# Two-layer perceiver, self-attention's maxima: bf16 parts instead of f32 rows, and zero products in the open sums

## What is computed

```python
x = x + L0_xattn(layernorm(x), ctx, mask, ...)       # 16 heads x 8, 2048 keys
x = x + L0_attn(layernorm(x), W_dq, W_uq, ...)       # causal: keys k <= query q
x = x + L0_ffn(layernorm(x), ...)
x = x + L1_xattn(layernorm(x), ctx, ctx, ...)
x = x + L1_attn(layernorm(x), attn_w, attn_b, ...)
x = x + L1_ffn(layernorm(x), ...)                    # 16 experts, 4 chosen

# L1_attn: masked scores are set to -10000 and kept in the softmax
scores = where(k <= q, k.q / sqrt(8), -10000.0); probs = softmax(scores, over k); out = probs @ v
```

## Time and profile before

| | us |
|---|---|
| median of 3 runs | 305.57 |
| lowest, highest | 305.34, 307.09 |
| the profiled execution's own time | 305.52 |
| its span | 303.5 |
| TensorE busy (share of the span) | 284.2 (94%) |
| VectorE busy | 227.0 (75%) |
| ScalarE busy | 206.4 (68%) |
| GpSimd busy | 68.7 (23%) |
| mean granted TensorE clock | 0.989 |

### The profile page before, as it was taken

One profiled execution on the slowest core, in us unless ns is written; L12 is line 12 of the kernel. 1 busy time (PEld: TensorE's weight loads), 2 busy tenths in 40 slices (PEclk: granted clock), 3 DMA queues, 4 the chain that ended last, 5 costly groups with the idle time before them and its releaser, 6 DMA issues.

```text
span 303.5 us, 10281 instructions
## 1 busy us (share of the span) xinstructions
PE 284.2 (94%) x4324; PEld 185.0 (61%) x4329; DVE 227.0 (75%) x371; ACT 206.4 (68%) x436; POOL 68.7 (23%) x135
## 2 busy tenths in 40 slices
PE   7957999999999999899989899999999999999995
PEld 5444666667676664453745567666666765436575
DVE  6944889999999983563638999999999970643583
ACT  5656689898998987524433698998989987133350
POOL 6793500110101003520000676001011021110001
PEclk9996999999999999999999999999999999999999
DMA  7973415532222450333100025522221100000000
GB/s 229 409 282 123 158 55 171 184 102 77 80 80 82 139 217 2 121 140 104 55 2 0 3 65 181 176 81 82 71 83 60 56 3 2 0 2 3 0 0 19
DMA packets 10898, 28.06 MB, mean 92 GB/s; under 512 B 2241, under 2 KB 3329, under 8 KB 10466
## 3 DMA queue, kind: packets, MB, share of 16 engines
q1 hardware_dynamic: 10776, 27.16, 26.6%
q10 hardware_dynamic: 74, 0.20, 0.2%
HBM read 20.74 MB, written 6.62 MB: 90 GB/s over the span
## 4 chain that ended last, share of the span: by engine, by line
PE 71%; DVE 15%; DMA 5%; ACT 3%; POOL 2%; issue 2%; SPq 1%; ACTq 1%; DVEq 0%; POOLq 0%
PE bank L1040 70%; DVE mx L812 10%; DMA ctxT_s<-in_ctxT 2%; DMA k_first_rows<-kparts 2%; DMA kpair<-k_first_rows 1%; ACT probs L545 1%; DVE s_neg L867 1%; POOL m_rows L427 1%; DVE negm L819 1%; ACTq L276 1%; DVE st L723 1%; DVE kparts L782 0%; PE bank L1336 0%; DVE k_rest L779 0%; POOL m_rows L429 0%
## 5 line engine op out<-in xcount | busy, mean ns | idle before, releaser
L812 DVE TENSOR_REDUCE mx<-bank 128x2 f32<-128x1024 f32 x128 | 153.0, 1222 | 16.1 <-PE bank L1040 12.7
L545 ACT ACTIVATE probs<-bank 128x512 f32<-128x512 f32 x256 | 139.3, 595 | 20.1 <-PE bank L1040 16.1
L1040 PE MATMUL bank<-q_exp,kpair 64*128 64x128 bf16 x1024 | 84.7, 218 | 1.9 <-ACT probs L545 1.2
L1040 PE MATMUL bank<-probs,v_all 128*9 128x128 f32 x2048 | 80.3, 274 | 1.1 <-ACT probs L545 1.0
L1040 PE MATMUL bank<-kpair,q_rows 64*128 64x512 bf16 x256 | 73.7, 387 | 5.6 <-DMA kpair<-k_first_rows 5.1
L1040 PEld LDWEIGHTS bank<-q_exp,kpair 64*128 64x128 bf16 x1024 | 55.3, 94 | 31.6 <-issue 12.7
L1040 PEld LDWEIGHTS bank<-probs,v_all 128*9 128x9 f32 x2048 | 43.2, 90 | 16.7 <-ACT probs L545 4.0
L427 POOL CAST m_rows<-negm 128x2 bf16<-128x2 f32 x32 | 6.9, 217 | 144.6 <-DVE negm L819 144.6
L1040 PEld LDWEIGHTS bank<-kpair,q_rows 64*128 64x128 bf16 x256 | 22.7, 93 | 7.4 <-issue 5.5
L482 ACT ACTIVATE v_all<-bank 128x512 f32<-128x512 f32 (+1 forms) x20 | 10.5, 539 | 13.3 <-PE bank L1040 13.3
L1040 PE MATMUL bank<-selq,ident_b 128*128 128x512 bf16 x70 | 17.8, 379 | 0.3
(11 more groups left out here) (219 smaller groups left out, 341.9 us busy)
## 6 DMA issues: line engine op xcount, KB each, us to landing
k_scratch<-kparts SPq DMA_DIRECT2D x24, 256.0 KB, 2.9
kpair<-k_scratch SPq DMA_DIRECT2D x62, 96.0 KB
kpair<-k_scratch SPq DMA_DIRECT2D x62, 64.0 KB
ctxT_s<-in_ctxT SPq DMA_DIRECT2D x4, 512.0 KB, 6.0
mask_s<-in_mask SPq DMA_DIRECT2D x2, 1024.0 KB, 10.3
kpair<-k_scratch SPq DMA_DIRECT2D x62, 32.0 KB
wM<-in_packM SPq DMA_DIRECT2D x1, 1728.0 KB, 7.0
wB<-in_packB SPq DMA_DIRECT2D x1, 599.0 KB, 5.0
```

The source lines that it names most:

```text
L545: act.activation(probs[:, j % 4, :], bank[:, 4 + j % 2, :], ACT.Exp).then_inc(S("exp_done"), 1)
L812: V.tensor_reduce(mx[n % 2][:, w, :], bank[:, 2 * (w % 2):2 * (w % 2) + 2, :], AX.X, ALU.max) \
L1040: return T.matmul(out_, lhsT=lhsT, rhs=rhs, start=start, stop=stop, **kw)
```

## The change

The maxima now go into a small contiguous f32 tile `s_neg` of 16 numbers a partition and batch. A new VectorE step `split_max(b)` splits them into three bf16 parts at stride 32 of a cleared bf16 tile `s_parts` (four operations on 128x16, each waiting for the one before). `neg_rows(b)` waits for the split and is four plain bf16 products with the bf16 identity; the three parts of a maximum land in three rows of its group, the 29 others are zero. `s_row` becomes bf16, `subtract(b)` a bf16 product that adds the three rows up. GpSimd clears `s_parts` and fills `ones_b` and `zero_b` in place of clearing `s_neg`. ScalarE's `exp_fill` reads the new `s_neg`.

On TensorE, `later(0, 0..2)` moves to the front and `neg_rows(0)` behind `scores(1)`; `later(1, 0..2)` moves ahead of `neg_rows(1)`. A new `hold(b, g, n)` adds n products of the zero tile with 512 columns of `selq` to an open sum: four after `later(0, 0..2)`, four after `later(1, 0..2)`, two after `turned(1, 0..2)`, in each of the two layers. On VectorE, `split_max(0)` stands behind `expand_k(l, 1)` and `split_max(1)` behind `s_max(1, 1)`.

```diff
-        s_neg = sb("s_neg", [P, B, 4 * (P + 1)])
-        s_row = wide[:, 6:8, :].rearrange("p b (j q) -> p b j q", j=4)
+        s_neg = sb("s_neg", [P, B, 4, 4])
+        s_rest = sb("s_rest", [P, B, 4, 4])
+        s_parts = sb("s_parts", [P, B, 4, P], BF16)
+        ones_b = sb("ones_b", [P, P], BF16)
+        zero_b = sb("zero_b", [P, P], BF16)
+        s_row = wide[:, 6, :].bitcast(BF16).rearrange("p (b j q) -> p b j q", b=B, j=4)
...
+        def part_of(b, k):
+
+            return s_parts[:, b, :, :].rearrange("p j (g r) -> p g j r", r=32)[:, :, :, k]
...
-                        pool.memset(s_neg[:, :, :], 0.0).then_inc(S("neg_zero"), 1)
+                        pool.memset(s_parts[:, :, :, :], 0.0).then_inc(S("neg_zero"), 1)
+                        pool.memset(ones_b[:, :], 1.0).then_inc(S("neg_zero"), 1)
+                        pool.memset(zero_b[:, :], 0.0).then_inc(S("neg_zero"), 1)
...
+                def split_max(b):
+
+                    if l == 0 and b == 0:
+                        dve.wait_ge(S("neg_zero"), 1)
+                    dve.wait_ge(S("s_neg"), 2 * l + b + 1)
+                    link(V.tensor_copy(part_of(b, 0), s_neg[:, b, :, :]))
+                    link(V.tensor_tensor(s_rest[:, b, :, :], s_neg[:, b, :, :], part_of(b, 0), ALU.subtract))
+                    link(V.tensor_copy(part_of(b, 1), s_rest[:, b, :, :]))
+                    V.tensor_tensor(part_of(b, 2), s_rest[:, b, :, :], part_of(b, 1), ALU.subtract) \
+                        .then_inc(S("s_split"), 1)
...
                 expand_k(l, 1)
+                split_max(0)
                 for i in range(2):
                     s_max(1, i)
+                split_max(1)
                 dve.wait_ge(S("neg_t"), 2 * l + 2)
...
                 def neg_rows(b):
 
-                    pe.wait_ge(S("s_neg"), 2 * l + b + 1)
+                    pe.wait_ge(S("s_split"), 2 * l + b + 1)
                     for j in range(4):
-                        last = T.transpose(bank[:, S_BANK[b][3], j * P:(j + 1) * P],
-                                           s_neg[:, b, j * P:(j + 1) * P], ident)
+                        last = mm(bank[:, S_BANK[b][3], j * P:(j + 1) * P], s_parts[:, b, j, :], ident_b[:, :])
                     last.then_inc(S("neg_t"), 1)
...
+                def hold(b, g, n):
+
+                    for _ in range(n):
+                        mm(bank[:, S_BANK[b][g], :], zero_b[:, :], selq[:, 0:512], start=False, stop=False)
+
                 def subtract(b):
 
                     for g in range(4):
-                        mm(bank[:, S_BANK[b][g], :], ones_sq[group(g), :],
+                        mm(bank[:, S_BANK[b][g], :], ones_b[group(g), :],
...
-                neg_rows(0)
+                if l == 0:
+                    pe.wait_ge(S("neg_zero"), 3)
+                later(0, range(3))
+                hold(0, 0, 4)
                 pe.wait_ge(S("k_s"), 2 * l + 2)
                 pe.wait_ge(S("q_s"), 2 * l + 2)
                 pe.wait_ge(S("v32"), 2 * l + 2)
...
                 mask(1, 0, range(4))
                 scores(1)
-                later(0, range(3))
+                neg_rows(0)
                 turned(0, range(3))
                 later(0, range(3, 4))
                 turned(0, range(3, 4))
                 subtract(0)
+                later(1, range(3))
+                hold(1, 0, 4)
                 neg_rows(1)
-                later(1, range(3))
                 turned(1, range(3))
+                hold(1, 0, 2)
                 later(1, range(3, 4))
                 turned(1, range(3, 4))
                 subtract(1)
```

More of the change, by code:

```diff
@@ L245, in x_before @@
             return len(X_UNIT) * l + sum(u < n for u in X_UNIT)
-        def s_max_of(b):
-            v = s_neg[:, b, :].rearrange("p (j r) -> p j r", j=4)[:, :, 0:P]
-            return v.rearrange("p j (g r) -> p g j r", r=32)[:, :, :, 0]
+        def part_of(b, k):
+            return s_parts[:, b, :, :].rearrange("p j (g r) -> p g j r", r=32)[:, :, :, k]
         def r_bank(k):
@@ L607, in exp_fill @@
                     act.activation(e_fill[:, b, :].rearrange("p (g j) -> p g j", g=4),
-                                   s_max_of(b), ACT.Exp,
+                                   s_neg[:, b, :, :], ACT.Exp,
                                    bias=B_("fill", 1)).then_inc(S("e_fill"), 1)
@@ L864, in s_max @@
                         dve.wait_ge(S("sa_done"), 2 * l + b + 1)
-                    if l == 0 and b == 0 and i == 0:
-                        dve.wait_ge(S("neg_zero"), 1)
-                    last = V.tensor_reduce(s_max_of(b)[:, 2 * i:2 * i + 2, :],
+                    last = V.tensor_reduce(s_neg[:, b, 2 * i:2 * i + 2, :],
                                            bank[:, S_BANK[b][2 * i]:S_BANK[b][2 * i] + 2, :].rearrange("p g (j k) -> p g j k", j=4),
@@ L871, in s_max @@
                         link(last)
-                        last = V.tensor_scalar(s_max_of(b), s_max_of(b), B_("nfill", 1), None, ALU.min)
+                        last = V.tensor_scalar(s_neg[:, b, :, :], s_neg[:, b, :, :], B_("nfill", 1), None, ALU.min)
                     if i:
                         last.then_inc(S("s_neg"), 1)
+                def split_max(b):
[7 more added lines that the diff above has]
+                        .then_inc(S("s_split"), 1)
                 def finish(b):
```

## The result

| | before | changed |
|---|---|---|
| first session: median, us (lowest, highest) | 305.70 (305.34, 307.09) | 308.77 (307.75, 309.43) |
| ratio, 95% interval | | 1.0091 [1.0065, 1.0117] |
| second session: median, us | 306.62 | 308.76 |
| ratio, 95% interval | | 1.0071 [1.0046, 1.0097] |
| span of the profiled execution, first and second session | 303.5 | 307.2, 305.4 |

The change made the kernel slower by 2 to 3 us where I had forecast 0.3 us less. The time is outside the range.

A forecast was written before the change was run, and what follows sets the result against it. TensorE's serial sequence in two self-attention stretches was taken as the bound; bf16 savings nearly all spent on 2.16 us of holds a layer left 0.12 + 0.18 = 0.30 us gained, so 305.3 us, range 304.3 to 306.7.

The forecast's parts named there:

- The place: TensorE's stretch in both self-attentions, 10.18 and 10.24 us; each microsecond earlier there is a microsecond off the end.
- the wait for v32: TensorE's wait for ScalarE's v32, 0.25 us in the first stretch and 0.31 in the second, was to go.
- the step of a zero product: Hold products on TensorE: 0.216 us each from the trace, 2.16 us for the ten of a layer.
- The 131 ns of the Trainium skill: Rejected price per 512-column hold product: ten would cost 1.31 us, gaining some 1.7 us more over both layers.
- The step that failed: End of each stretch: exponentials start no later than before, so the values' products, reaching the last group 1.6 us in, follow TensorE.
- the last of the signs of being wrong: Values' products that start on time while their end waits for ScalarE's exponentials; listed as showing the forecast wrong.
- 10.06: Forecast stretch up to the values' products, us, from 10.18 and 10.24: gains of 0.12 and 0.18.
- The subtractions of batch 0 with what follows: Batch 0's last turned product and bf16 subtractions, with batch 1's masks starting beside: 1.07 us, bounds 1.07 and 1.40.
- The split's 0.84 us: VectorE's four split operations: 0.84 us, bounds 0.7 and 1.4; batch 0's was to fall into 1.45 us of idleness.
- the turns' +0.28: Upper bound on four bf16 turns of the maxima: 0.60 us against 0.32 taken, twice a layer.
- the subtractions' +0.33 and +0.12: Upper bounds on the last turned product with bf16 subtractions: 1.40 against 1.07 and 1.40 against 1.28, once a layer each.
- a fallen clock: Rival: a wait of microseconds drops TensorE to 1.2 GHz in a stretch, 308.6 us and more; chance 0.05.

The follow-up runs named there:

- Experiment 4: Changed kernel without holds, split_max(0) ahead of expand_k(l, 1), subtractions of groups 0 to 2 ahead of the last masks and turned product; ratio 1.0009 against the kernel before.
- experiment 8: Changed kernel without its first four holds (after the first twelve masks); stretches 13.03 and 13.29 us in one profile, against 13.17 and 13.29 with all holds.
- experiment 9: Changed kernel with split_max(0) ahead of expand_k(l, 1) and only four holds, behind batch 1's first masks; ratio 1.0017 in both runs; also reviews clock falls without holds.
- experiment 2: Changed kernel with all ten holds of each layer taken out; ratio 0.9972 against the kernel before, stretches 11.63 and 12.00 us.
- experiment 5: Changed kernel without holds, early subtractions, first half of batch 0's split ahead of the keys' expansion, the rest behind; 304.77 us, ratio 0.9961 against the kernel before.
- experiment 6: Changed kernel with early subtractions, batch 0's split halved around the keys' expansion, one zero product behind the first twelve masks; ratio 0.9964 against the kernel before.

## Why the prediction was wrong

**What held.** The place (two stretches, all serial behind them), the clock (1.00 in both with the holds, 0.989 over all), the bf16 turns (0.32 each, predicted 0.32), no wait ahead of the turns of batch 1, the wait for v32 gone. The trace was right about the step of a zero product: the second four take 0.87 us, 0.86 predicted. The 131 ns of the Trainium skill (TensorE: Matmul & The Clock Gate, Back-to-back issue gap) would have made them 0.52, and these rows do not agree with it.

**The step that failed.** "ScalarE's exponentials start no later than before, and the values' products reach the last group 1.6 us after their start, so they follow TensorE." I let the bf16 subtractions of groups 0 to 2, which run beside the turned product of group 3, signal ScalarE at once. Their completion reaches it 1.16 us after that product's start, as late as with f32 (1.17). So the 0.65 us saved behind it in batch 1 brought the values' products forward and not the exponentials: the values' products lengthened from 1.89 to 2.38 us in layer 0 and 2.37 in layer 1. That is 0.49 us a layer. Experiment 4 takes the mechanism away and has them back at 1.89. Values' products whose end waits for the exponentials are the last of the signs of being wrong that I had written down myself. The rows of the kernel before do not give it away:

```profile
141.93 0.69 PE L1040 MATMUL bank<-v_all,k_s 32*128 32x512 f32 x1
141.93 0.70 PE L1040 MATMUL bank<-mask_s,ones_sq 32*128 32x512 f32 x3
...
142.47 1.44 PE L1040 MATMUL bank<-mask_s,ones_sq 32*128 32x512 f32 x5
```

The first exponential starts at 143.10, when the turned product is done, but an f32 subtraction has a second record at 142.47 and is done no sooner itself. What the sum lacked was the question which of the two ScalarE waited for; nearly half of each layer's miss hangs on it, 0.49 of 1.00 us in layer 0 and 0.48 of 1.12 in layer 1.

**Terms that were mis-sized**, layer 0. Up to the values' products I had 10.06; from the first mask it was 10.48 (135.69 to 146.17), and it began 0.09 us later than I had put it. The subtractions of batch 0 with what follows: 1.07 taken, 1.27 measured, as the next masks did not start beside the last step but 0.31 us after it (141.13 to 141.44); this lies within the bounds I had given. First hold 0.86, measured 0.97 (136.05 to 137.02); last hold 0.43, measured 0.53: both stand ahead of 32-row or 32x32 products and cost 0.1 us more than their steps, while the second hold, behind the same masks but ahead of full-array turns, took 0.87. These three make 0.41 of the 0.42 us. The sum is -0.12 + 0.42 + 0.09 + 0.49 = +0.88, as measured. In layer 1 the slow split of batch 0 adds a wait of 0.12 us: -0.18 + 0.42 + 0.09 + 0.48 + 0.12 = +0.93, measured +0.94.

**A price that was wrong and nearly harmless.** The split's 0.84 us came from rows where GpSimd was idle; beside GpSimd its first cast takes 1.04 alone, and the whole split of batch 0 in layer 0 takes 1.76 (136.50 to 138.26), that of batch 1, with GpSimd idle, 0.93. The holds hid that in layer 0. Take them away and it is what TensorE waits for (experiment 8).

**The range** was too narrow by its own bounds: the turns' +0.28 four times, the subtractions' +0.33 and +0.12 twice each make 2.0 us, or 307.3, and I had written 306.5 and 306.7. What I had left out came on top with the same sign. The measured 308.8 falls by its number among the times that I had kept for a fallen clock, but the clock did not act in the changed kernel (1.00 in both stretches). It fell where holds were missing and TensorE waited for 1 us more (experiment 9). In experiments 2, 5 and 6, with none or one of the holds, the clock did not fall in 36 executions: the ten holds are a price paid against something that did not happen there.

## What to carry to other kernels

A filler product costs its full time unless TensorE would wait just there, so size each against the wait it stands in and leave it out elsewhere. When a product gets faster, ask which earlier product in program order its semaphore still waits behind, and whether the engine that reads the bank then becomes the bound; moving the fast products ahead of the slow one gave back 0.21 us here. And price a small VectorE cast or two-input operation with GpSimd's work beside it, not from a place where GpSimd is idle.

## What the runs showed of the hardware that I had not expected

- The completion of a 0.4 us bf16 product on its own quarter of the array reached ScalarE 1.16 us after its start, behind an f32 product issued before it on another quarter; issued ahead of that product, it came 0.41 us after its start.
- A 128x16 cast took 1.04 us beside a GpSimd product and 0.20 alone; a 128x512 product of VectorE took 1.56 and 0.69; and GpSimd's own took 1.59 beside it and 1.04 when it began first.
- Without fillers and with a wait of 1.06 us between short bursts, the mean granted clock was 0.978 or less in 9 of 24 executions; in the one of them that was profiled it fell to 1.2 GHz for nearly all of 8.93 us. Without that wait the mean was 0.983 or more in all of 36. That the wait is the cause is likely and not shown.
- A group of four zero products took 0.87 us ahead of full-array products and 0.97 ahead of 32x32 ones.
